# Second attention of a four-stage block: unrolled slots, one rounding pass, gate inside the scales

## The reference

```
def _dyn_quant(x):                       # per row
    s = max(max|x| / 127, 1e-8);  q = clip(round(x / s), -127, 127)
def _w8a8_linear(x, w, b):               # w quantised per output row
    return einsum(qx, qw) * (sx * sw) + b
x_n = layernorm(x)                       # eps 1e-5
q = _w8a8_linear(x_n, wq, bq)            # 16 heads of 32
k = cond @ wk.T + bk;  v = cond @ wv.T + bv      # 64 context rows per batch
attn = softmax(q k^T / sqrt(32) + mask)
x = x + tanh(g_xattn[1]) * _w8a8_linear(attn v, wo, bo)
```

## Time and profile before

| | TensorE | VectorE | ACT | POOL |
|---|---|---|---|---|
| busy in the span, us | 1969.8 | 1150.6 | 1045.7 | 989.2 |

### The profile page before, as it was taken

How to read it: one execution, slowest core, us unless ns; L and a number is a source line. 1 busy time by engine, 2 the same in 40 slices (tenths; PEclk the granted TensorE clock), 3 DMA queues, 4 the chain that set the end, 5 groups by cost and what they waited for, 6 DMA issues and landing times. The chain is left out here.

```text
span 2272.5 us, 29205 instructions
## 1 busy us (share of the span) xinstructions
PE 1969.8 (87%) x9812; PEld 1410.0 (62%) x9850; DVE 1150.6 (51%) x2272; ACT 1045.7 (46%) x2189; POOL 989.2 (44%) x902
## 2 busy tenths in 40 slices
...
GB/s 133 47 2 1 10 29 20 1 10 1 29 20 1 10 10 19 1 1 1 1 128 47 24 15 100 170 235 231 183 190 233 3 3 2 1 28 10 24 20 24
DMA packets 71074, 114.59 MB, mean 50 GB/s; under 512 B 7552, under 2 KB 35072, under 8 KB 70224
## 3 DMA queue, kind: packets, MB, share of 16 engines
q1 hardware_dynamic: 63760, 95.95, 12.6%
...
...
## 5 line engine op out<-in xcount | busy, mean ns | idle before, releaser
L578 POOL TENSOR_TENSOR a_xcl<-xT,a_xch 128x512 fp32r<-128x512 f32 x64 | 82.5, 1289 | 477.5 <-ACT a_xch L447 477.5
L517 DVE TENSOR_REDUCE a_nmax<-a_S 128x1 f32<-128x192 f32 (+3 forms) x256 | 139.0, 553 | 255.2 <-PE a_S L653 252.7
L709 PE MATMUL a_A<-a_pT,a_vf 128*128 128x512 f32 (+1 forms) x448 | 234.9, 606 | 1.3 <-ACT a_pT L460 1.2
L652 PE MATMUL a_S<-a_kT,a_qT 128*128 128x288 f32 (+3 forms) x640 | 213.9, 433 | 3.0 <-ACT a_pr_even L450 1.7
L110 PE MATMUL a_A<-a_wlo,a_xch 128*128 128x512 f32 x256 | 152.6, 596 | 12.1 <-DVE a_qb L540 9.4
L450 ACT ACTIVATE a_pr_odd<-a_S,a_nmax 128x320 f32<-128x320 f32 (+1 forms) x128 | 80.9, 633 | 178.2 <-DVE a_nmax L517 176.5
L460 ACT ACTIVATE a_pT<-a_TR 128x512 f32<-128x512 f32 (+1 forms) x224 | 133.0, 594 | 61.8 <-PE a_TR L699 61.8
L652 PEld LDWEIGHTS a_S<-a_kT,a_qT 128*128 128x128 f32 x640 | 120.8, 192 | 55.1 <-issue 27.6
L450 ACT ACTIVATE a_pr_even<-a_S,a_nmax 128x192 f32<-128x192 f32 (+1 forms) x128 | 66.9, 525 | 154.3 <-DVE a_nmax L517 154.2
L671 PE MATMUL a_A<-a_wkv,xT 128*128 128x256 f32 x512 | 134.8, 386 | 0.6 <-DMA a_wkv<-in_L_xattn_wv_dram 0.6
L1308 POOL TENSOR_TENSOR e_wlo<-expert_raw,e_whi 128x1408 fp32r<-128x1408 f32 x32 | 103.5, 3255 | 68.3 <-ACT e_whi L1381 68.3
...
## 6 DMA issues: line engine op xcount, KB each, us to landing
...
```

The costliest lines, as they stand in the source:

```text
L517: ve.tensor_reduce(nmax[:, s % 2, i:i + 1], pair(s, i), AX.X, ALU.max, negate=True).then_inc(s_max, 1)
L578: pool.tensor_tensor(xcl[:, t % 2], xT[:, :, tok(t)], xch[:, t % 2].bitcast(F32), ALU.subtract).then_inc(xlo_ready, 1)
L652: pe.matmul(bank[:, lo:hi], qT[:, t % 2, hq], kT[:, par(t), lo:hi], start=True, stop=hi < nk)
L709: last = pe.matmul(A[:, A_USE["V", t, 0][0]], vf[r, par(t), i], pT[r, i % 2], start=i == 0, stop=i == nkt - 1)
```

## The change

*Rounding.* Instead of adding MAGIC and taking it off again, ROUND = 1.5 x 2^23 + 0x6600 is added. The lower 16 bits of the 32-bit sum are then the half-precision number 1536 + n. `low_half` reads them as such, every second 16-bit value of the tile; the transpose on TensorE takes them so, and the copy out of PSUM takes 1536 off. In the attention that copy is on VectorE (`x`, `o`), in the setup on ACT. The FFN, whose xq and hq were 16-bit numbers rounded with 1536, gets the same; these tiles become 32-bit.

*Scales.* The normalisation is not carried out: ACT centres (`c`, cx = mean - x), and since the quantisation divides by the row's maximum, only the floor needs the deviation, which POOL gives as two powers (`p`). ACT puts the row's scale on q (`i`) and, when it copies the transposed q, scale and bias of its column (`k`, four instructions), which are now one value per partition; 1/sqrt(32) is in them. Values get two columns of ones (vbd is 66 wide), so P x V also gives the row sums; VectorE divides 512 outputs (`N`) instead of 1024 probabilities on POOL. The gate is multiplied into the scale row `gsw` and the bias `gbo` in setup; POOL adds gbo to x beforehand (`B`) and y at the end (`A`).

*Order.* All is unrolled. `walk` goes through slots -3 to 17 and gives each engine the words of its ORDER; a word such as P1 means piece 1 of operation P, for the tile slot + AHEAD. P, t and V are in two halves. TensorE: T transpose of xq, Q product with wq, K transpose of q, S scores, P transpose of the probabilities, V product with values, U transpose of oq, Y product with wo. ACT: c, v (variance), q (quantise), i, k, e (Exp), t (copy of P), O (quantise output). VectorE: b (statistics), m (maximum and scales), x, D (mask), M (maximum), N, o, Y. POOL: B, s (subtract maximum), p, A.

*Loads.* bq, bo and all of the mask (2048 rows of 256 B) are loaded in the attention's setup behind the weights, where VectorE waits for them before it writes kbd. w3 of the FFN is loaded in the FFN's setup.

```diff
+BIG = 1536.0
+ROUND = 12582912.0 + 0x6600
+def low_half(ap):
+    return ap.bitcast(F16).rearrange("p (n two) -> p n two", two=2)[:, :, 0]
...
-                        quantise(ve, c, wi[:, w, o], raw[:, 2 + w, o], inv[:, w, o:o + 1], scratch[:]).then_inc(quant_ready, 1)
+                        ve.tensor_scalar(wi[:, w, o], raw[:, 2 + w, o], inv[:, w, o:o + 1], ROUND, ALU.mult, ALU.add).then_inc(quant_ready, 1)
...
+                ve.wait_ge(const_ready, 4)
+                ve.wait_ge(bias_loaded, 80)
...
+    PE_ORDER = "S0 U0 P0 Q0 P1 T0 Y0 V0 K0 V1"
+    ACT_ORDER = "q0 t0 i0 t1 c0 v0 k0 e0 O0"
+    DVE_ORDER = "b0 D0 o0 M0 x0 Y0 N0 m0"
+    POOL_ORDER = "B0 s0 p0 A0"
+    AHEAD = {"PE": {"T": 2, "Q": 1, "K": 1, "S": 0, "P": -1, "V": -1, "U": -2, "Y": -2},
+             "ACT": {"c": 3, "v": 3, "q": 2, "i": 1, "k": 1, "e": 0, "t": -1, "O": -1},
+             "DVE": {"b": 3, "m": 3, "x": 2, "D": 0, "M": 0, "N": -1, "o": -2, "Y": -2},
+             "POOL": {"B": 2, "p": 3, "s": 0, "A": -2}}
...
+    def walk(engine, order, do):
+        for slot in range(-3, NT + 2):
+            for word in order.split():
+                s = slot + AHEAD[engine][word[0]]
+                if 0 <= s < NT:
+                    do(word[0], int(word[1]), s)
...
+                    if name == "B":
+                        pool.wait_ge(cx_ready, s + 1)
+                        pool.tensor_tensor(x[:, s], x[:, s], gbo[:], ALU.add).then_inc(biased, 1)
+                    if name == "p":
+                        pool.wait_ge(var_ready, s + 1)
+                        if s > 1:
+                            pool.wait_ge(m_ready, 2 * (s - 1))
+                        pool.tensor_tensor(root[:, u], var[:, u], half[:], ALU.pow).then_inc(root_ready, 1)
+                        pool.tensor_tensor(unroot[:, u], var[:, u], mhalf[:], ALU.pow).then_inc(root_ready, 1)
+                    if name == "s":
+                        pool.wait_ge(max_ready, s + 1)
+                        pool.tensor_tensor(p[:, u], p[:, u], pm[:, u].unsqueeze(2).broadcast_to([P, H1, T]), ALU.subtract).then_inc(centred, 1)
+                    if name == "A":
+                        pool.wait_ge(y_ready, s + 1)
+                        pool.wait_ge(biased, s + 1)
+                        pool.tensor_tensor(x[:, s], x[:, s], y[:, u], ALU.add).then_inc(x_done, 1)
...
+                    if name == "c":
+                        act.wait_ge(mean_ready, s + 1)
+                        if s > 1:
+                            act.wait_ge(xq_ready, s - 1)
+                        act.activation(cx[:, u], x[:, s], ACT.Identity, bias=mv[:, u, 0:1], scale=-1.0).then_inc(cx_ready, 1)
...
+                    if name == "q":
+                        act.wait_ge(m_ready, 2 * s + 1)
+                        if s > 1:
+                            act.wait_ge(xq_turned, s - 1)
+                        act.activation(xq[:, u], cx[:, u], ACT.Identity, bias=big[:], scale=rec[:, u]).then_inc(xq_ready, 1)
+                    if name == "i":
+                        act.wait_ge(q_full, s + 1)
+                        act.wait_ge(m_ready, 2 * (s + 1))
+                        if s > 0:
+                            act.wait_ge(q_turned, s)
+                        act.activation(qs[:], QY[:], ACT.Identity, scale=sx[:, s % 4]).then_inc(qs_ready, 1)
+                    if name == "k":
+                        act.wait_ge(q_turned, s + 1)
+                        if s > 1:
+                            act.wait_ge(sc_full, s - 1)
+                        for g in range(KD):
+                            last = act.activation(qT[:, u, g], QT[:, g], ACT.Identity, bias=bq[:, g:g + 1], scale=sq[:, g:g + 1])
+                        last.then_inc(q_copied, 1)
+                    if name == "e":
+                        act.wait_ge(centred, s + 1)
+                        act.activation(p[:, u], p[:, u], ACT.Exp).then_inc(exp_done, 1)
+                    if name == "t":
+                        act.wait_ge(p_turned, 2 * s + n + 1)
+                        if s > 0:
+                            act.wait_ge(o_full, 2 * (s - 1) + n + 1)
+                        act.activation(pT[:, HALF * n:HALF * n + HALF], PT[:], ACT.Copy).then_inc(p_copied, 1)
...
+                    if name == "O":
+                        act.wait_ge(o_ready, s + 1)
+                        if s > 1:
+                            act.wait_ge(oq_turned, s - 1)
+                        act.activation(oq[:, u], o[:, u].rearrange("p j h d -> p (j h d)"), ACT.Identity, bias=big[:], scale=reco[:, u]).then_inc(oq_ready, 1)
...
+                    if name == "m":
+                        ve.wait_ge(cx_ready, s + 1)
+                        link(ve.tensor_reduce(am[:, u:u + 1], cx[:, u], AX.X, ALU.max, apply_absolute_value=True))
+                        ve.wait_ge(root_ready, 2 * (s + 1))
+                        link(ve.tensor_scalar(mx[:, u:u + 1], am[:, u:u + 1], 1.0 / 127.0, root[:, u], ALU.mult, ALU.max))
+                        if s > 1:
+                            ve.wait_ge(xq_ready, s - 1)
+                        ve.reciprocal(rec[:, u], mx[:, u:u + 1]).then_inc(m_ready, 1)
+                        if s > 3:
+                            ve.wait_ge(qs_ready, s - 3)
+                        ve.scalar_tensor_tensor(sx[:, s % 4], mx[:, u:u + 1], unroot[:, u], floor[:], ALU.mult, ALU.mult).then_inc(m_ready, 1)
+                    if name == "x":
+                        ve.wait_ge(xq_turned, s + 1)
+                        if s > 1:
+                            ve.wait_ge(q_full, s - 1)
+                        ve.tensor_scalar(xqT[:, u].rearrange("p k t -> p (k t)"), TB[:, 0], BIG, None, ALU.subtract).then_inc(xq_copied, 1)
+                    if name == "D":
+                        ve.wait_ge(sc_full, s + 1)
+                        if s > 1:
+                            ve.wait_ge(p_turned, 2 * (s - 1))
+                        ve.tensor_tensor(p[:, u], SC[:], mask[:, s].unsqueeze(1).broadcast_to([P, H1, T]), ALU.add).then_inc(sc_read, 1)
+                    if name == "M":
+                        ve.wait_ge(sc_read, s + 1)
+                        ve.tensor_reduce(pm[:, u], p[:, u], AX.X, ALU.max).then_inc(max_ready, 1)
+                    if name == "N":
+                        ve.wait_ge(o_full, 2 * (s + 1))
+                        link(ve.reciprocal(inv[:], O[:, :, 2 * D1:2 * D1 + 2]))
+                        if s > 1:
+                            ve.wait_ge(oq_ready, s - 1)
+                        link(ve.tensor_tensor(o[:, u], O[:, :, 0:2 * D1].rearrange("p j (h d) -> p j h d", h=2),
+                                              inv[:].unsqueeze(3).broadcast_to([P, H1 // 2, 2, D1]), ALU.mult))
+                        link(ve.tensor_reduce(amo[:, u:u + 1], o[:, u].rearrange("p j h d -> p (j h d)"), AX.X, ALU.max, apply_absolute_value=True))
+                        link(ve.tensor_scalar(so[:, u], amo[:, u:u + 1], 1.0 / 127.0, FLOOR, ALU.mult, ALU.max))
+                        ve.reciprocal(reco[:, u], so[:, u]).then_inc(o_ready, 1)
+                    if name == "o":
+                        ve.wait_ge(oq_turned, s + 1)
+                        if s > 1:
+                            ve.wait_ge(y_full, s - 1)
+                        ve.tensor_scalar(oqT[:, u].rearrange("p k t -> p (k t)"), TB[:, 1], BIG, None, ALU.subtract).then_inc(oq_copied, 1)
+                    if name == "Y":
+                        ve.wait_ge(y_full, s + 1)
+                        if s > 1:
+                            ve.wait_ge(x_done, s - 1)
+                        ve.scalar_tensor_tensor(y[:, u], QY[:], so[:, u], gsw[:], ALU.mult, ALU.mult).then_inc(y_ready, 1)
...
+                    if name == "V":
+                        pe.wait_ge(p_copied, 2 * s + n + 1)
+                        if s > 0:
+                            pe.wait_ge(o_ready, s)
+                        if n == 0 and s + 3 < NT:
+                            pe.wait_ge(m_ready, 2 * (s + 4))
+                        for j in range(HALF * n, HALF * n + HALF):
+                            last = pe.matmul(O[:, j, 0:STAT], pT[:, j], vbd[:, b, j], start=True, stop=True)
+                        last.then_inc(o_full, 1)
...
+                    if name == "U":
+                        pe.wait_ge(oq_ready, s + 1)
+                        tb_free("U", s)
+                        for k in range(KD):
+                            last = pe.transpose(TB[:, 1, k * P:(k + 1) * P], low_half(oq[:, u, k * P:(k + 1) * P]), ident_h[:])
...
-        xq = s_.sb("xq", [P, 2, 2, D], F16)
+        xq = s_.sb("xq", [P, 2, 2, D])
...
-        hq = s_.sb("hq", [P, 2, F1], F16)
+        hq = s_.sb("hq", [P, 2, F1])
...
-                ve.memset(big[:], BIG).then_inc(const_ready, 1)
+                ve.memset(big[:], ROUND).then_inc(const_ready, 1)
...
```

(26 more changed lines are left out.)

411 lines of the change are left out of this document (172 added, 239 removed).

## The result

| | before | after |
|---|---|---|
| median of 4 runs each (us) | 2272.34 | 2201.53 |
| lowest to highest | 2270.27 to 2276.45 | 2199.32 to 2202.91 |
| span of the profiled execution | 2272.5 | 2199.4 |
| mean granted TensorE clock | 0.927 | 0.945 |

The ratio is 0.9685, with a 95% interval of 0.9669 to 0.9702: 70.8 us less, where I forecast 51 (2221, range 2210 to 2250).

The account below looks back on a forecast made before the run. VectorE was taken to set the pace in the second attention's middle (96.65 of 104 us busy). Attention ending 50.7 us earlier, FFN unchanged: 2274.25 - 50.7 = 2223.5, profiled 2.3 above the median, so 2221 us, range 2210 to 2250.

Parts of the forecast that it names:

- the loop through both engines: Attention: D, o on VectorE, Y, V0, K, V1 on TensorE, N, m, b on VectorE set the period; sum 9.8 us.
- the clock charge: Attention: TensorE's lower clock adds 2.5 us in the second slot and 5 for one later drop.
- the fill: Attention's start, first bn_stats to end of tile 0's P x V: 33.3 us, against 33.95 before.
- Rivals A: Attention: the clock falls in half the slots, 15.1 us each instead of 9.9; 2252 us, chance 0.12.
- C: TensorE stays at 1.2 GHz through the attention, slower than before; 2292 us, chance 0.03.
- One slot: Attention's steady period, the longest loop through the engines' lists: 9.9 us, fifteen periods 148.5 us.
- Rival D: Attention: small VectorE steps overlap more, so the period is 9.3 us; 2212 us, chance 0.09.
- Setup and start: Before attention's statistics: setup 2.0 us shorter, bo loaded earlier; first bn_stats at 1719.2 instead of 1726.92.
- The mask's wait: Attention setup: VectorE waits 1.5 us for the mask load before writing kbd, ends 0 and 11.7.
- Drain: Attention's end: last slots lack b, m, Q and T, -3.5 us; 8.8 us follow the last tile's V1.
- rival B: FFN: strided weight loads are slow, costing 2 to 27 us over 16 tiles; middle 2238, chance 0.12.
- ACT's four copies: Attention: four 128-column scaled copies take 1.3 us together (0.6 to 2.4); any delay to S is absorbed waiting for O.

Follow-up runs that it names:

- warm kernel: Identity transposes added in TensorE's waits at both ends of the attention, against the kernel with reordered engine lists: 2169.36 us, ratio 0.9552 to before.

## Why the prediction was wrong

*Where the time came from* was read rightly: VectorE's passes behind POOL, TensorE's waits for POOL, the load of bo. The shape of the slot, the loop through both engines, also came out: the kernel with m moved and one input taken off, and the one with plain copies, move as that loop says; with m moved alone the loop missed POOL's hold on one small step (9.65 us for 8.7). What failed is the size of three terms of the sum, all to the same side: the clock charge, the fill and the slot.

*Clock* (+7.5 charged, nothing measured). I took a drop of 5 us and a slow second slot from a stage with waits of 3 us, though the same group has the full clock kept after 1.64 us. The new slot has three waits (0.59, 0.76 and 0.30 us) where I forecast one of 1.3, and its middle stands at 1.00. The runs say how far that is from a loss: with 0.24 us waited ahead of P0 the clock is kept, with 2.21 us it is lost in every second slot, and a loss costs 1.3 us rather than 5. They do not give a longest wait that is safe, since the kernel with one rounding pass more loses the clock in two slots whose longest wait is 1.3 us. Rivals A and C needed slots at the lower clock, and none of the middle slots has it.

*Fill* (33.3 forecast, 27.63). To the first mask addition it was right, 15.4 us against the 14.95 of my pieces, and so was the way from there to the end of Exp (6.7 against 6.5). Then I put the end of the next scores, the two halves of P, Q, T, V0, K and V1 at the slow clock, 11.3 us. In the trace Exp ends at 1739.66 and V1 at 1745.20, 5.5 us, and from P0 on (1740.79) all are at the full clock. My own rows held this: the P x V product at 1758.87 took 2.00 us in the old fill, which is the full clock. The warm kernel shows the same from the other side. The sum has a slip too: my pieces add up to 32.75, not 33.3.

*One slot* (9.9 forecast, 9.26), the largest single term, 9.7 us over 15 periods. I added busy durations, and neighbours on one engine overlap. From start to start the pieces are, forecast first: D 1.16, 1.15; o and the hop 0.69, 0.78; Y 0.9, 0.86; V0 1.0, 0.84; K 0.53, 0.44; V1 and hop 1.15, 1.04; N 2.17, 2.02; m 1.22, 1.18; b 1.0, 0.95. All but o and the hop are too long, V0, V1 and N most (0.11 to 0.16), and rounding 9.82 up added 0.08. Rival D (9.3 us, 2212) had the size of the slot, and I gave it 0.09; it put all of it down to VectorE's small steps, while more than half of the excess is on TensorE (Y, V0, K and V1, 0.40 of 0.56). All three errors are needed to get from 2221 to 2201.5.

*Setup and start* held: -8.3 for -7.7. The mask's wait of 1.5 us didn't come, the lower end of its range, and the rest of the setup gave 0.9 less than forecast, so the near hit is in part luck. *Drain*: half of the shortening I credited, since the clock falls in the last slots as waits grow (after a wait of 3.04 us the halves of P take 1.06 and 1.09 us instead of 0.61 and 0.63). *FFN*: rival B is out; the 16-bit tiles give the same times. (Its 2238 stood on the profiled sum; from 2221 its middle is 2236.) By the rule of the Trainium skill on strides (SBUF — State Buffer, the note on cachelines under "Door 1") the FFN would lose nothing, and the trace agrees, 98 ns for both. The FFN's 1.07 us over before is not from them: with the same FFN it takes 241.8 us from its first constant to the end in the kernel with one rounding pass more, as before the change, 242.8 in the kernel after and 243.6 in the one with the row sum, so it varies by over 1 us without an edit to it.

*ACT's four copies* were put at 1.3 us and take 1.50. They delay S by 0.76, and that is absorbed ahead of U, as the forecast said and the kernel with plain copies shows.

How the slots' gain divides between the edits is settled only in part. A 512-wide rounding pass where POOL is busy costs 1.36 us a slot; a row sum or one POOL pass in the new lists costs next to nothing; a second POOL pass costs 1.9 at the full clock and 2.6 with the clock's losses. These prices hold in the new order. What each would be worth in the old one was not tried, so how much of the gain is due to the new order by itself is not shown.
